# Values of four heads projected at once, batch after batch, in a causal attention; two reorderings in a grouped attention

## The reference, cut to what matters

```python
# layer 0: 16 heads of 128, batch 2, sequence 1024, model width 256, causal
q = jnp.einsum('bsd,hed->bhse', x, W_Q)
k = jnp.einsum('bsd,hed->bhse', x, W_K)
v = jnp.einsum('bsd,hed->bhse', x, W_V)
scores = jnp.einsum('bhse,bhme->bhsm', q, k) * scale
scores = jnp.where(causal, jnp.float32(-1000000000.0), scores)
pattern = jax.nn.softmax(scores, axis=-1)
z = jnp.einsum('bhsm,bhme->bhse', pattern, v)
out = jnp.einsum('bhse,hde->bsd', z, W_O)
x = _layernorm(x + out)
...
# layer 1: 16 query heads of 16, 4 key heads, no mask
scores = jnp.einsum('bqhd,bkhd->bhqk', q, k) / HD
prob = jax.nn.softmax(scores, axis=-1)
out = jnp.einsum('bhqk,bkhd->bqhd', prob, v).reshape(b, s, D)
```

## Time and profile before

| what | value |
|---|---|
| time, median of 3 runs | 2382.63 us (2374.97 to 2385.11) |
| the profiled execution | 2378.21 us |
| its span, first to last instruction | 2376.4 us |
| PE busy | 2183.7 us, 92% |
| DVE busy | 1543.6 us, 65% |
| ACT busy | 1194.5 us, 50% |
| POOL busy | 550.0 us, 23% |
| mean granted TensorE clock | 0.95 of full speed |

### The profile page before, as it was taken

How to read it: one execution, slowest core, us unless ns; L and a number is a source line. 1 busy time by engine, 2 the same in 40 slices (tenths; PEclk the granted TensorE clock), 3 DMA queues, 4 the chain that set the end, 5 groups by cost and what they waited for, 6 DMA issues and landing times. The chain is left out here.

```text
span 2376.4 us, 35246 instructions
## 1 busy us (share of the span) xinstructions
PE 2183.7 (92%) x11264; PEld 1644.4 (69%) x11264; DVE 1543.6 (65%) x2607; ACT 1194.5 (50%) x2397; POOL 550.0 (23%) x547
## 2 busy tenths in 40 slices
PE   5999999999999999869999859999998589999996
PEld 4888888888888888738878733333334368877885
DVE  4666666666666666647656648888881536645665
ACT  4555555555555555434334323777776234433442
POOL 2333333333333333202222100000000012222220
PEclk9999999999999999969999966999999679999998
DMA  2000000000000000001111020000000011111111
GB/s 67 17 15 13 15 15 15 15 15 15 15 15 15 15 15 3 1 19 48 52 41 47 22 44 16 16 21 17 19 15 5 1 46 46 47 47 40 47 53 45
DMA packets 43155, 61.70 MB, mean 26 GB/s; under 512 B 8347, under 2 KB 23494, under 8 KB 43078
## 3 DMA queue, kind: packets, MB, share of 16 engines
q1 hardware_dynamic: 43078, 60.71, 9.2%
HBM read 50.59 MB, written 2.10 MB: 22 GB/s over the span
## 5 line engine op out<-in xcount | busy, mean ns | idle before, releaser
L1360 POOL TENSOR_TENSOR a_pr<-a_pr,a_rinv 128x128 f32<-128x128 f32 (+7 forms) x256 | 293.8, 1148 | 598.4 <-DVE a_rinv L1597 598.4
L1042 DVE TENSOR_REDUCE a1m_negm<-psum 128x1 f32<-128x1024 f32 x256 | 302.9, 1220 | 59.4 <-PE psum L920 58.7
L1023 ACT ACTIVATE a1m_pt<-psum 128x512 f32<-128x512 f32 x512 | 266.2, 602 | 93.6 <-PE psum L935 93.4
L647 DVE SCALAR_TENSOR_TENSOR f_hid<-psum,f_bias_now,f_act_s 128x512 f32<-128x512 f32 x168 | 126.0, 750 | 267.4 <-ACT f_act_s L604 195.9
L604 ACT ACTIVATE f_act_s<-psum,f_bias_now 128x512 f32<-128x512 f32 x168 | 115.7, 689 | 339.1 <-PE psum L71 264.0
L504 POOL TENSOR_TENSOR f_lo_gu<-f_raw_gu,f_hi_gu 128x512 fp32r<-128x512 f32 x84 | 109.0, 1298 | 750.3 <-ACT f_hi_gu L579 750.3
L1524 ACT ACTIVATE a_pth<-psum 128x512 fp32r<-128x512 f32 (+3 forms) x384 | 174.7, 490 | 193.1 <-PE psum L1416 192.1
L69 PE MATMUL psum<-xh,f_hi_gu 128*128 128x512 f32 x672 | 266.2, 396 | 2.0 <-POOL f_lo_gu L504 1.4
L71 PE MATMUL psum<-xh,f_lo_gu 128*128 128x512 f32 x672 | 264.3, 393 | 0.0
L70 PE MATMUL psum<-xl,f_hi_gu 128*128 128x512 f32 x672 | 263.7, 392 | 0.0
L1517 ACT ACTIVATE a_pr<-psum,a_negm 128x128 f32<-128x128 f32 (+7 forms) x256 | 190.3, 744 | 62.9 <-DVE a_negm L1588 62.7
(11 more groups left out here) (221 smaller groups left out, 4910.2 us busy)
## 6 DMA issues: line engine op xcount, KB each, us to landing
f_raw_gu<-in_gu SPq DMA_DIRECT2D x84, 256.0 KB, 2.7
a_wr<-in_qkv SPq DMA_DIRECT2D x32, 384.0 KB, 3.0
f_raw_dn<-in_down SPq DMA_DIRECT2D x84, 128.0 KB, 2.0
a_qq<-a_qhi SPq DMA_DIRECT2D x128, 32.0 KB, 1.9
yT<-in_xT SPq DMA_DIRECT2D x4, 512.0 KB, 7.2
a_wor<-in_o SPq DMA_DIRECT2D x16, 128.0 KB, 2.0
a_qq<-a_qlo SPq DMA_DIRECT2D x64, 32.0 KB, 1.9
out<-n_xn SPq DMA_DIRECT2D x4, 512.0 KB, 2.9
```

The costliest lines, as they stand in the source:

```text
L1023: act.activation(pt[:, s % SLOTS, g, :], st_ps[:, n % 3, :], ACT.Exp, scale=1.0 / HD1).then_inc(exp_done, 1)
L1042: dve.tensor_reduce(negm[:, u % 2, g * NQ + q:g * NQ + q + 1], mx_ps[:, bank, :, :], AX.XY, ALU.max, negate=True).then_inc(mx_taken, 1)
L1360: pool.tensor_tensor(pr[:, j, 0:n], pr[:, j, 0:n], rinv[:, j:j + 1].to_broadcast([P, n]), ALU.mult).then_inc(p_done, 1)
```

## The change

**First attention.** `prepare` is gone: the loads of x and its splitting move into the attention's block, behind the first head's q and k weights, and x of batch 1 is split in units 4 and 5 of half 0. The halves are now `hb` = 16 * batch + head. The hardware loop is gone; all 32 halves are written out. v is made for four heads at once (`VG`), without transposing: x is the stationary operand and the 512 columns of four heads' weights the moving one, one task of 6 matmuls for each tile of 128 tokens, eight such tasks in the units of every fourth half (a lead half). The weights of v come apart, 4 pieces of 128 KB for four heads, and their low part is one POOL instruction of 1024 columns (`split_v`, in unit 5 of the third half of four, behind the division of tile 6). The tasks of a half are dealt out anew: k (chunk 0) from unit 1 to 3, q (chunk 1) from 3 to 5, k (chunk 1) from 4 to 6, `pv` (chunk 0) from unit 6 to 4, the first of two `o` from 7 to 6. The output weights are split once a half, not once a head. `pv` of chunk 1 waits for the last low part only ahead of the key tiles that need it.

```diff
-    HB = 2 * H0
+    HB = B * H0
+    VG = 4
-    PLAN = [[("pv", 1, True)],
-            [("q", 0), ("k", 0)],
-            [("o", 1, True, 0)],
-            [("o", 1, True, 1), ("q", 1)],
-            [("k", 1), ("vt", 0)],
-            [("vt", 1), ("v", 0)],
-            [("pv", 0, False), ("v", 1)],
-            [("o", 0, False, 0), ("o", 0, False, 1)]]
+    def plan(hb):
+        first, last, lead = hb == 0, hb == HB - 1, hb % VG == 0
+        units = [[] if first else [("pv", 1, True)],
+                 [] if last else [("q", 0)],
+                 [] if first else [("o", 1, True, 0)],
+                 ([] if first else [("o", 1, True, 1)]) + ([] if last else [("k", 0)]),
+                 [("pv", 0, False)],
+                 [] if last else [("q", 1)],
+                 ([] if last else [("k", 1)]) + [("o", 0, False, 0)],
+                 [("o", 0, False, 1)]]
+        if lead:
+            for qt in range(NQ):
+                units[qt].append(("v", qt))
+        if last:
+            units.append([("pv", 1, False), ("o", 1, False, 0), ("o", 1, False, 1)])
+        return units
+    PRE = [("q", 0), ("k", 0), ("q", 1), ("k", 1)]
...
+            load(0)
+            load_x(0)
+            load_x(1)
+            load_v(0)
+            load(1)
+            load_o(0)
+            load_x(2)
+            load_x(3)
...
+            split(0)
+            split_v(0)
+            normalise(0, 0)
+            split(1)
+            split_o(0)
+            for hb in range(HB):
                 for qt in range(NQ):
+                    if after(hb, qt + 1)[0] < HB:
+                        normalise(*after(hb, qt + 1))
+                    if qt == 2 and hb + 2 < HB:
+                        split(hb + 2)
+                    if qt == 4 and hb >= 1:
+                        split_o(hb)
+                    if qt == 5 and hb % VG == 2 and hb + 2 < HB:
+                        split_v(hb // VG + 1)
...
+                elif kind == "v":
+                    if c == 0:
+                        pe.wait_ge(wvl_done, hb // VG + 1)
+                    x0 = hb // H0 * S + c * P
+                    for dt in range(DT):
+                        i = mm3(pe, o, xh[:, dt, x0:x0 + P], xl[:, dt, x0:x0 + P], wvh[:, dt, :], wvl[:, dt, :],
                                 dt == 0, dt == DT - 1)
-                elif kind == "v":
-                    pe.wait_ge(task_out, done_by(hb, ("vt", c)))
-                    for q in range(CQ):
-                        i = pe.transpose(o[:, q * P:(q + 1) * P], vt[:, c, q * P:(q + 1) * P], ident[:])
```

```diff
                         for k in range(2):
                             if ahead:
                                 maxima(*ahead, k, bank)
+                            if k == 1 and i % 2 == 1 and u * NK + i // 2 >= LAG:
+                                values(u * NK + i // 2 - LAG)
                             scores(u, i, k)
-                        if i % 2 == 1 and u * NK + i // 2 >= LAG:
-                            values(u * NK + i // 2 - LAG)
...
-                        if i == TURN + 1 and u < LAST:
+                        if i == TURN and u < LAST:
                             keep_maxima(u + 1)
```

More of the change, by code:

```diff
@@ L1224, in causal_attention @@
+    PRE = [("q", 0), ("k", 0), ("q", 1), ("k", 1)]
+    WHOLE = ("o",)
+    PLANS = [plan(hb) for hb in range(HB)]
+    FLAT = [[(-1, t) for t in PRE]] + [[(hb, t) for unit in PLANS[hb] for t in unit] for hb in range(HB)]
+    PLACE = {key: k for k, key in enumerate(key for row in FLAT for key in row)}
+    HIS = {}
+    for key in PLACE:
+        if key[1][0] not in WHOLE:
+            HIS[key] = len(HIS)
     NB = CQ + 2 * (NQ - CQ)
@@ L1459, in task @@
-                i.then_inc(task_done, 1)
-            def half(hb, h, b, first, last):
-                k, n = bases(hb)[0], 0
-                for qt, tasks in enumerate(plan(first, last)):
-                    if qt < NQ - 2:
-                        scores(hb, b, qt + 2)
-                    elif not last:
-                        scores(hb + 1, 1 - b, qt + 2 - NQ)
-                    turn(hb, qt)
-                    for t in tasks:
-                        task(hb, h, b, t, k + n, bank_of(b, first, n))
-                        n += 1
@@ new lines, in task @@
+                i.then_inc(task_done, 1)
+            pe.wait_ge(ident_done, 1)
+            for t in PRE:
+                task((-1, t))
+            pe.wait_ge(rounded, 2)
+            for qt in range(2):
+                scores(0, qt)
+            for hb in range(HB):
+                for qt, tasks in enumerate(PLANS[hb]):
+                    if qt < NQ:
+                        if after(hb, qt + 2)[0] < HB:
+                            scores(*after(hb, qt + 2))
+                        turn(hb, qt)
+                    for t in tasks:
+                        task((hb, t))
@@ L1540, in task @@
                 act.wait_ge(task_done, k + 1)
[L1541 to L1551 removed]
+                act.activation(pair_of(key)[0], r_ps[:, k % 2, :], ACT.Copy,
+                               scale=SCALE if key[1][0] == "q" else 1.0).then_inc(task_hi, 1)
@@ new lines, in _ @@
+            round_weights(0)
+            round_x(0)
+            round_x(1)
+            for t in PRE[:2]:
+                task((-1, t))
+            act.wait_ge(mask_set, 1)
+            act.activation(mask[:], mask0[:], ACT.Copy).then_inc(rounded, 1)
+            act.activation(idr[:], ident[:], ACT.Copy).then_inc(rounded, 1)
+            for t in PRE[2:]:
+                task((-1, t))
+            round_v(0)
+            for qt in range(2):
+                soften(0, qt)
+            round_weights(1)
@@ L1552, in half @@
+            round_o(0)
+            for hb in range(HB):
+                for qt, tasks in enumerate(PLANS[hb]):
+                    if qt < NQ:
+                        keep_hi(hb, qt)
+                        if after(hb, qt + 2)[0] < HB:
+                            soften(*after(hb, qt + 2))
                     for t in tasks:
                         if t[0] not in WHOLE:
-                            task(b, t, k + n, bank_of(b, first, n))
-                        n += 1
-                    if qt == 3:
-                        if not isinstance(hb, int) or hb < HB - 2:
-                            round_weights(b, (h + 2) * 16)
-                        if b == 0 and not first:
-                            round_o(h)
@@ L1576, in end @@
-            def end():
-                k = bases(HB - 1)[0] + sum(len(u) for u in plan(False, True))
-                task(0, ("pv", 1, True), k, k % 2)
-            walk(act, half, begin, end)
+                            task((hb, t))
+                    if hb == 0 and qt in (4, 5):
+                        round_x(qt - 2)
+                    if qt == 1 and hb + 2 < HB:
+                        round_weights(hb + 2)
+                    if qt == 4 and hb >= 1:
+                        round_o(hb)
@@ new lines, in _ @@
+            keep_x(0)
+            keep_x(1)
+            for t in PRE:
+                task((-1, t))
+            for qt in range(2):
+                maximum(0, qt)
+            invert(0, 0)
+            for hb in range(HB):
+                for qt, tasks in enumerate(PLANS[hb]):
+                    if qt < NQ:
+                        if after(hb, qt + 1)[0] < HB:
+                            invert(*after(hb, qt + 1))
+                        if after(hb, qt + 2)[0] < HB:
+                            maximum(*after(hb, qt + 2))
+                        keep_lo(hb, qt)
+                    if hb == 0 and qt in (4, 5):
+                        keep_x(qt - 2)
+                    for t in tasks:
+                        task((hb, t))
```

433 lines of the change are left out of this document (156 added, 277 removed).

## The result

The changed kernel takes 2345.43 us (median of 4 runs, 2339.7 to 2356.63), the kernel before 2383.87 (2374.97 to 2389.52): a ratio of 0.9837, 95% interval 0.9801 to 0.9873. The forecast was 2334 with a range of 2303 to 2362; it holds the time, which lies 11 us above the point. The profiled execution of the changed kernel took 2343.43 us, span 2341.7, 34.7 less than before.

What follows compares the result with a forecast made beforehand. PE was taken to bound the first attention; the second's bound needed its event order read. Savings of 35.0 and 9 us, 44.0 together, came off the profiled 2378.2 us: 2334 us, range 2303 to 2362.

Steps and rivals of the forecast that it cites:

- wait at pv: First attention: PE's 0.33 us wait each half for DVE to add the second o to yT goes; 10.1 us saved.
- start: First attention: first matmul near 9.2, unit 1's transposes at about 24.6, 14.5 us earlier; 1.4 given back, 13.1 us saved.
- unrolling: First attention's loop written out: the branch costs nothing and longer instruction streams show no cost, so 0 us.
- (a): First attention, halves without v: cover only even with the DVE, ACT, DVE, POOL chain; 0.2 us each, 5 us lost.
- (b): First attention, lead halves: v's task in unit 6 waits 0.7 us for k's result, 8 times; 6 us lost.
- (c): First attention: split_v, 2.4 us on POOL, pushes tile 7's division by about 0.7 us, 7 times; 5 us lost.
- end: First attention: the last half's pv, two units earlier, no longer fills the wait of its last tiles; 0.7 us lost.
- Copy: Second attention's turn: ACT's copy of the maxima ahead of two exponentials, step 11 starts 1.5 us after the turn; 1.1 less.
- Values: Second attention: values ahead of the last score tile only move the wait to the third tile; period stays 2.61, 2 lost.
- filled-wait rival: Second attention: values do fill the score tile's wait, the double step falls to about 2.4 us; 2302 us, chance 0.12.
- the chain did not become the bound: First attention rival: the chain becomes the bound, each half waits 2.0 us, kernel slower at 2391 us; chance 0.07.
- short cover: First attention rival: cover runs short, the chain is late by 1 us more a half; 2365 us, chance 0.14.

Runs made afterwards that it cites:

- added groups: Changed kernel plus groups of four constant transposes: 62 ahead of q tasks, ratio 0.990; or 64 at the scores of tiles 2 and 6, 2368.82 us.
- all repairs: Changed kernel with x chunks moved, v's tasks in units 6 and 7 earlier, v weights' low part in pieces, values back behind last score tile: 2320.65 us.
- the kernel with the later x chunks: Changed kernel with rounding of x's third and fourth chunk moved from two units of half 0 to four units of half 4: 2334.04 us, ratio 0.9776.

## Why the forecast held, and where it was off

**The bound.** PE sets the pace of the first attention, and what leaves its stream leaves the time: right. PE is idle 2.1% of the stretch that I had read before, under the 3% from which I called the forecast wrong; over the whole stage, with its start and last half, it is 3.1%, so that sign was stated too loosely to decide anything.

**The sum of the first attention, term by term.** Forecast 35.0, measured 24.4.

| term | forecast | measured | from |
|---|---|---|---|
| transposes of v | 28.5 | 26.0 | 62 x 0.42, added groups |
| wait at pv | 10.1 | 10.1 | absent after |
| start | 13.1 | 11.6 | 39.12 - 26.12 - 1.4 |
| clock behind unit 1 | none | -0.6 | 12.0 us to tile 4's transposes, 11.4 where it stayed up |
| unrolling | 0 | 2.5 | 31 x 0.08 |
| (a) halves without v | -5 | -2.6 | see below |
| (b) lead halves | -6 | -10.1 | tasks in another order |
| (c) POOL's v weights | -5 | -2.4 | in pieces, 7 x 0.34 |
| later x chunks | none | -3.3 | moved, 3.1 to 3.5 |
| end | -0.7 | -1.4 | last half |

(a) is what a half without v has over 30.24 - 0.33 - 0.84 - 12 x 0.23 - 0.08 = 26.2: it takes 26.3, 24 x 0.11. The end is what the stage takes behind the mark of half 30, 38.70 us for 39.83, where what left PE's stream would make it 2.5 shorter. The terms add up to 29.8, 5.4 more than measured. A lead half has 0.4 to 0.5 us more than 48 matmuls of 0.23 even with all repairs (33.36 + 30.81 - 2 x 26.31 = 11.55, against 11.1), over eight of them 3 to 4 us; its cause and the last 2 us are open.

The steps that failed are these. **Term (b)** was right in kind and too small, 10.1 for 6: I priced the wait of unit 6 (0.7, measured 0.73) and did not follow v's last task over the border of the half, where its reader stands. **An edit that I had not costed:** it is on record that x of batch 1 is split in units 4 and 5 of half 0, but the sum has no term for it. It stands there with DVE waiting for ACT in front of each chunk, and costs 3.3. **The 0.4 to 0.5 that a lead half costs beyond its matmuls** had no term either. **(a) and (c)** were too high, by 5.0 together: the cover over the chain held better than my 0.2 a half, and only 0.3 of POOL's 2.4 us reach PE. **The start** lost 1.5 by a fall of the clock that I had not allowed for. From the first matmul on the clock rose as before (4.4 us after it; before 4.3), but fell again from 20.6 to 27.4. In the four profiles where it did not, unit 1's transposes come at 23.3 to 24.1, ahead of my 24.6. The old start varies too, 37.2 to 39.1 in four profiles, and the one that I read was the latest. **The loop** was put at nothing and cost 2.5.

**The second attention.** Copy: step 11 starts 1.46 us after the turn's first transpose, as forecast (1.5), also with the copy alone moved. By itself that should have given 1.1 a unit, 15.4; it gave 0.93, 13.0. Values: the period stays at 2.61, the wait goes to the third tile, the filled-wait rival is out. With the turn's new place they cost 0.26 a unit with the copy moved (21.95 against 21.69), 14 x 0.26 = 3.7, where I took 0.33 x 14 + 2 = 6.6. So 9.3 a stage for a forecast of 9, with both parts smaller than I took: the sum is nearer than its parts by luck. The mark shows 5.9, because the unit after the first took 24.54 us (22.54 before): its clock rose later, 58 us after the stage's first matmul in place of 47. The same code took 21.58 there in the kernel with the later x chunks, so this differs between profiles of the same code. But four of the six profiles with both edits have the late rise, and none of the others with all maxima made; whether the change makes it likelier is open.

**The rivals.** The cover did not run short, the chain did not become the bound, and the start came nearly as early as forecast. My reason against the short cover, that DVE, ACT and POOL all get less work a half, holds for DVE alone: by the rows of 100 to 300 us ACT has 17.5 us a half before and 17.6 now, POOL 11.9 both times, since the output weights are now split every half. The excess over 2334 is 10.6 of the first attention and 3.1 of the second, less the 1.1 and 3.3 us of stretches with the same code; the median then lies 2.0 above the profiled execution.

## What to carry to other kernels

When work is moved or cut into pieces, list for each piece the unit that it now stands in on every engine, and follow its result to the first reader, across the border of the loop's body: the two terms that I missed in this way were worth 7 us more than I had taken, and moving a few lines gave back 13. Where three tasks of a unit share two banks, the third waits for the result of the first: put the longest (here v) second. In this ring of three banks, changing the order of its users left the period at 2.61 us; a fourth bank brought a unit from 21.95 to 17.76, with the maxima left out. Before a gain of a few us is put down to an edit, look at a mark that stands ahead of it.

## What the runs showed of the hardware

- Less work for PE can cost time: with the maxima left out and three score banks, the granted clock was 0.53 in the second attention and the kernel took 2533.1 us, against 2320.04 with a fourth bank and a clock of 1.00 (one run each).
- The clock also makes executions of one kernel differ: the kernel with v's tasks in another order took 2330 and 2331 us at a mean clock of 0.949, 2346 and 2347 at 0.940 and 0.938. Between profiles with the same code it differs at the end of the second attention by 11 us (81 or 92), at its start by 5.7 (the first two units 47.6 or 53.3), at the start of the first attention by up to 3.4 (tile 4's transposes at 34.75 or 38.13), and by 1.2 to 1.4 for each short dip behind a wait of 1.17.
- The loop over heads cost 0.17 us a pass, in two parts of 0.08 at the output projection of each half and not at the branch.
